# A MetaFormer block on one core: the attention's product with kv apart from wout, in column strips of PE, and all places of the convolution's work among the feed-forward chunks laid down anew

## The chip, the cores and the metric

One core of a Trainium2 chip. The metric is device microseconds of one execution: before, the median of three runs is 750.94 us (750.56 to 751.97). Everything is float32, or float32r where the kernel splits a number into a high and a low part.

## The reference, cut to what matters

x is 4 images of 96 channels and 56 x 56 pixels. A deformable attention with depthwise convolutions is added to x, then a mixture of experts over the pixels (all four experts are computed, the two best gates are kept).

```python
value = dwconv(xn, w_v, stride=1)
query = dwconv(xn, w_q, stride=1).reshape(B * 12, 32, 3136)
key   = dwconv(xn, w_k, stride=2).reshape(B * 12, 32, 784)
offset = gelu(layernorm(dwconv(xn, w_off1, stride=2))) @ w_off2
v_sampled = grid_sample(value, tanh(offset + ref)).reshape(B * 12, 32, 784)
attn = einsum('bcm,bcn->bmn', query, key) * SCALE      # no softmax
out  = einsum('bmn,bcn->bcm', attn, v_sampled)
x = x + einsum('bchw,oc->bohw', out, w_out)
t = tokens(x)
t = t + sum_e gate[e] * (gelu(layernorm(t) @ w1[e] + b1[e]) @ w2[e] + b2[e])
```

Without a softmax the attention of a head is query times the 32 x 32 matrix kv = key times v_sampled. The reshape puts 8 channels of four image quarters into the 32 "channels" of a head, so kv joins the four quarters, and is masked so that channels of different heads don't meet.

## The kernel before, in words

**Layout.** A picture's channels lie as 3 blocks of 32; a block's partitions are 4 quarters x 32 channels. `query[:, i, :]` is block i, 128 partitions by 784 pixels. There are 28 token tiles of 112 pixels, 7 groups of four of them (448 pixels) for the experts, 8 sample tiles of 98, and 8 strips of 392 pixels for the attention (two per quarter).

**Attention of batch b.** `sample` (DVE) weighs the gathered value rows into `vs`. `key_values` (PE) makes kv for each quarter q of the output, `mask_kv` (DVE) masks it, `mixes` (PE) multiplies it by wout: for each quarter three matrices `mix[:, q, i, :]` of 128 x 96, emptied by ACT. `attended` (PE) then makes each strip of y with three matmuls over the blocks, `add_y` (DVE) adds it to x, and `x1_to_tokens` (PE) turns it into tokens that ACT empties.

**Experts.** A chunk is 128 hidden units of one expert for 448 pixels: three float32r products into `ph` (L762 to L764), gelu on ACT (L1006), and the second product into `py` (L746). Three chunks make an output: DVE adds the bias and multiplies by the gate into one of four buffers `ye` (L1416), and POOL adds `ye` into x, the first 76 by an accumulating DMA (L1480). There are 84 chunks and 28 outputs per batch, 252 chunks in this form; the last 84 use split hidden values. The chunks of batch b-1 run while batch b is convolved.

**What sets the order.** Each engine has its own program, written out by hand: lists say how many chunks (`CHUNKS_AHEAD`, PE), gelus (`GELUS_AHEAD`, ACT), outputs (`OUTPUTS_AHEAD`, DVE) and sums (`SUMS_AHEAD`, POOL) stand ahead of each piece of the convolution's work. `chunks_to(plan.at("kv"))` issues chunks up to that number and then goes on. Each engine runs its program strictly in that order.

**Waits between them.** PE's second product of the first chunk of output n waits until output n-2 is made (two banks `py`):

```python
pe.wait_ge(ye_ready, FREE_OUTPUTS + n - 1)      # second(k), L745; k // 3 is n
```

DVE's output n waits until sum n-4 has landed (four buffers `ye`), and a sum waits for its output and for the sums before it:

```python
after_sums(dve, n + 1 - EXPERTS)                # outputs_to
pool.wait_ge(ye_ready, FREE_OUTPUTS + n + 1)    # add_outputs, L1476
after_sums(pool, n)
```

POOL also gathers the value rows for the samples, two indirect DMAs for each of 8 sample tiles (L1469), once the positions are known and the value table has been written to memory by DMA. The table is written after the last valT job; `values_to_tokens` makes valT with seven jobs on PE and ACT. POOL's loop over a batch, L1491 to L1495:

```python
for k in range(NS):
    add_outputs(added, SUMS_AHEAD[b][k])
    added = SUMS_AHEAD[b][k]
    gather(b, k)
```

SP loads the gates and stores the results (`load_gates`, `store_result`) behind the same semaphores. DVE's convolution taps (L1133) run over `xpad` in SBUF.

Of the kernel before, what the change touches and what calls it, by code (L numbers as in the profile page):

```python
# [35 lines left out]
SP = 98  # L36
# [31 lines left out]

def act_jobs():

    order = jobs(0, "xT", NG) + jobs(0, "pad", 2 * BLOCKS) + jobs(0, "offT", 2) + jobs(0, "valT", QT)[:VALUE_HALF] + jobs(0, "offc", 2) + jobs(0, "valT", QT)[VALUE_HALF:]
    order += jobs(1, "xT", NG)[:EARLY_SLOTS] + jobs(0, "keyT", 2) + jobs(1, "xT", NG)[EARLY_SLOTS:] + jobs(0, "mix", QUARTERS) + jobs(0, "x1T", NG) + jobs(1, "pad", 2 * BLOCKS)
    order += jobs(0, "gateT", 1) + jobs(1, "offT", 2) + jobs(1, "offc", 2)
    for b in range(1, BATCH):
        more = b + 1 < BATCH
        order += jobs(b, "valT", QT)
        if more:
            order += jobs(b + 1, "xT", NG)
        order += jobs(b, "keyT", 2)
        if more:  # L80
            order += jobs(b + 1, "pad", 2 * BLOCKS)
        order += jobs(b, "mix", QUARTERS) + jobs(b, "x1T", NG)
        if more:
            order += jobs(b + 1, "offT", 2)
        order += jobs(b, "gateT", 1)
        if more:
            order += jobs(b + 1, "offc", 2)
    return order


def dve_jobs():

    order = jobs(0, "offs", 1)
    for b in range(BATCH):
        order += jobs(b, "kv", QUARTERS) + jobs(b, "y", NY) + jobs(b, "x1c", NG)
        if b + 1 < BATCH:
            order += jobs(b + 1, "offs", 1)
# [17 lines left out]
SCALE_AFTER = 4  # L115
# [3 lines left out]
    dict(x1c=(0, 0, 0, 0, 3, 3, 4), gateT=(3,), offT=(10, 10), offc=(16, 16), offs=(18,)),  # L119
    dict(valT=(42, 42, 43, 43, 44, 44, 45), xT=(45, 46, 46, 47, 47, 48, 48), keyT=(49, 49),  # L120
         pad=(69, 69, 70, 71, 71, 72), kv=(72, 72, 73, 73), mix=(73, 73, 74, 74), y=(74, 74, 74, 74, 74, 74, 74, 74),
         x1T=(74, 74, 74, 74, 74, 74, 75), offT=(75, 76), x1c=(80, 80, 81, 82, 86, 86, 87), gateT=(86,), offc=(93, 93),
         offs=(95,)),
    dict(valT=(118, 118, 119, 119, 120, 120, 121), xT=(121, 122, 122, 123, 123, 124, 124), keyT=(125, 125),
         pad=(145, 145, 146, 147, 147, 148), kv=(148, 148, 151, 151), mix=(151, 151, 152, 152),
         y=(152, 152, 152, 152, 152, 152, 152, 152), x1T=(152, 152, 152, 152, 152, 152, 153), offT=(153, 154),
         x1c=(158, 158, 159, 160, 164, 164, 165), gateT=(164,), offc=(172, 172), offs=(174,)),
    dict(valT=(198, 198, 199, 199, 200, 200, 201), keyT=(204, 204), kv=(222, 226, 233, 233), mix=(233, 233, 234, 234),
         y=(234, 234, 234, 234, 234, 234, 234, 234), x1T=(234, 234, 234, 234, 234, 234, 235),
         x1c=(241, 241, 243, 243, 249, 249, 250), gateT=(249,)),  # L130
# [3 lines left out]
    dict(x1n=(0, 0, 0), x1c=(0, 0, 0, 0, 3, 3, 4), exp=(0,), gateT=(3,), offT=(10, 10), offc=(16, 17), tanh=(19,)),  # L134
    dict(valT=(42, 42, 43, 43, 44, 44, 45), xT=(45, 46, 46, 47, 47, 48, 48), keyT=(49, 49), xn=(67, 69, 69),
         pad=(69, 70, 70, 71, 71, 72), mix=(73, 73, 74, 74), x1T=(74, 74, 74, 74, 74, 74, 75), offT=(75, 76),
         x1n=(78, 80, 82), x1c=(80, 81, 83, 84, 86, 86, 87), exp=(81,), gateT=(86,), offc=(93, 94), tanh=(95,)),
    dict(valT=(118, 118, 119, 119, 120, 120, 121), xT=(121, 122, 122, 123, 123, 124, 124), keyT=(125, 125),
         xn=(143, 144, 145), pad=(145, 146, 146, 147, 147, 148), mix=(151, 151, 152, 152),
         x1T=(152, 152, 152, 152, 152, 152, 153), offT=(153, 154), x1n=(156, 158, 160),  # L140
         x1c=(158, 159, 161, 162, 164, 164, 165), exp=(159,), gateT=(164,), offc=(172, 173), tanh=(175,)),
    dict(valT=(198, 198, 199, 199, 200, 200, 201), keyT=(204, 204), mix=(233, 233, 234, 234),
         x1T=(234, 234, 234, 234, 234, 234, 235), x1n=(239, 241, 243), x1c=(241, 242, 245, 245, 249, 249, 250),
         exp=(243,), gateT=(249,)),
# [43 lines left out]
def build(nc, t, out):  # L188
# [4 lines left out]
    with ExitStack() as ctx:  # L193
# [11 lines left out]
        head_mask = sb("head_mask", [C, C])  # L205
# [290 lines left out]
        def _(pe):  # L496
# [127 lines left out]
            def key_values(b, quarters, before=lambda q: None):  # L624

                keyq = keyT[:, :, :].rearrange("p (q h) c -> p h q c", h=2)
# [8 lines left out]
            def mixes(b, before=lambda q: None):  # L635

                for q in range(QUARTERS):
                    before(q)
                    pe.wait_ge(dve_done, dved(b, "kv", q))
                    bank = act_bank(b, "mix", q)  # L640
                    for i in range(BLOCKS):
                        last = nc.tensor.matmul(bank[:, i * C:(i + 1) * C], kv[:, q, i, :, :].rearrange("d k c -> d (k c)"), wout[:, :], start=True, stop=True)
                    last.then_inc(act_full, 1)
# [51 lines left out]
            def first_rest(b, plan, chunks_to):  # L695
# [11 lines left out]
                key_values(b, range(QUARTERS))  # L707
                mixes(b)
# [8 lines left out]
            def rest(b, with_head, plan, chunks_to):  # L717
# [7 lines left out]
                key_values(b, range(QUARTERS), lambda q: chunks_to(plan.at("kv", q)))  # L725
                mixes(b, lambda q: chunks_to(plan.at("mix", q)))
# [811 lines left out]
```

## Time and profile before

| | |
|---|---|
| median of three runs | 750.94 us |
| profiled execution | a span of 749.4 us from the first to the last instruction; the page gives no other time of it |
| PE busy | 707.8 us (94%), mean granted clock 0.985 |
| DVE busy | 582.8 us (78%) |
| ACT busy | 384.5 us (51%) |
| POOL busy | 216.9 us (29%) |

Busy times of PE are modelled: shown matmuls overlap, and costs are better read from one start to the next. The stages are: batch 0 alone up to about 138 us, then three cycles of about 160 us (batches 1, 2 and 3 among the chunks of the batch before), and from about 637 us the last chunks alone.

### The profile page before, as it was taken

The numbers are of one execution on the slowest core, as the hardware profiler recorded it, in microseconds if no ns is written. First come the engines' busy times: TensorE is split into PE (matmuls) and PEld (weight loads), VectorE is DVE, ScalarE is ACT, GpSimd is POOL, SyncE is SP. The second block draws the span as 40 slices with busy tenths as digits, with TensorE's granted clock in tenths as the row PEclk, the third lists the DMA queues.
The fourth block names the chain that finished last, engine by engine and source line by source line (L and its number), as shares of the span: only waits on it lengthen the run. The fifth ranks groups of instructions, "written<-read, shape, count | busy, mean of one in ns | idle before, by whom it ended". The sixth has DMA issues, their size and how long they took to land.

```text
span 749.4 us, 9619 instructions
## 1 busy us (share of the span) xinstructions
PE 707.8 (94%) x3186; PEld 495.8 (66%) x3186; DVE 582.8 (78%) x1511; ACT 384.5 (51%) x722; POOL 216.9 (29%) x184
## 2 busy tenths in 40 slices
PE   5798999799999999999999999999998999999996
PEld 5556566566676666556767566666664665788884
DVE  4889648899999858699999477899975275677774
ACT  2314124744464614744556218545542256899995
POOL 4001700012128610111168201222285121344443
PEclk9998999799999999999999999999999999999999
DMA  8007200044464530345654422435645201121111
GB/s 195 9 0 198 53 9 1 7 98 86 89 185 115 98 56 10 68 103 119 155 129 83 86 48 46 82 80 101 190 102 109 35 20 49 47 69 51 66 47 37
DMA packets 29697, 58.66 MB, mean 78 GB/s; under 512 B 6224, under 2 KB 20176, under 8 KB 29360
## 3 DMA queue, kind: packets, MB, share of 16 engines
q0 software_dynamic: 11584, 17.90, 15.4%
q1 hardware_dynamic: 14336, 32.59, 14.7%
q10 hardware_dynamic: 3728, 7.55, 3.3%
q8 instruction: 26, 0.43, 0.2%
q14 instruction: 23, 0.19, 0.1%
HBM read 30.30 MB, written 14.65 MB: 60 GB/s over the span
## 4 chain that ended last, share of the span: by engine, by line
PE 56%; DVE 19%; DMA 7%; ACT 6%; POOL 5%; issue 5%; POOLq 0%; ACTq 0%
PE py L746 9%; PE pd L662 8%; PE ph L578 7%; DVE val L1133 6%; POOL big L1469 4%; DMA xbuf<-ye 4%; DVE query L1133 3%; PE pa L650 3%; PE pa L529 2%; PE ph L762 2%; PE ph L782 2%; PE ph L784 2%; PE ph L763 2%; PE ph L783 2%; PE ph L764 2%
## 5 line engine op out<-in xcount | busy, mean ns | idle before, releaser
L746 PE MATMUL py<-hid,w 128*96 128x448 f32 x504 | 234.4, 546 | 11.5 <-ACT hid L1006 8.7
L1006 ACT ACTIVATE hid<-ph,b 128x448 f32<-128x448 f32 x252 | 158.9, 632 | 148.1 <-PE ph L764 144.8
L762 PE MATMUL ph<-x_hi,w_hi 96*128 96x448 f32 x252 | 164.4, 653 | 0.0
L1480 POOL DMA_DIRECT2D xbuf<-ye x76 | 66.6, 877 | 327.2 <-DMA xbuf<-ye 163.2
L1469 POOL DMA_INDIRECT big<-value_table,rows x64 | 87.8, 1372 | 90.5 <-DVE rows L1193 56.5
L746 PEld LDWEIGHTS py<-hid,w 128*96 128x96 f32 x504 | 81.6, 165 | 31.2 <-ACT hid L1006 12.6
L763 PE MATMUL ph<-x_lo,w_hi 96*128 96x448 f32 x252 | 93.5, 371 | 0.0
L764 PE MATMUL ph<-x_hi,w_lo 96*128 96x448 f32 x252 | 92.8, 368 | 0.0
L1482 POOL TENSOR_TENSOR xbuf<-xbuf,ye 96x448 f32<-96x448 f32 x36 | 53.9, 1497 | 102.6 <-DVE ye L1416 99.9
L1416 DVE SCALAR_TENSOR_TENSOR ye<-py,b,gate_all 96x448 f32<-96x448 f32 x112 | 75.3, 674 | 9.3 <-PE py L746 7.3
L1443 DVE TENSOR_TENSOR hid_lo<-hid,hid_hi 128x448 fp32r<-128x448 f32 x84 | 59.7, 710 | 27.3 <-ACT hid L1015 27.1
L1133 DVE SCALAR_TENSOR_TENSOR query<-xpad,conv_w,query 128x784 f32<-128x784 f32 x80 | 78.3, 1027 | 0.5
L1133 DVE SCALAR_TENSOR_TENSOR val<-xpad,conv_w,val 128x784 f32<-128x784 f32 x80 | 78.3, 1026 | 0.4
L762 PEld LDWEIGHTS ph<-x_hi,w_hi 96*128 96x128 f32 x252 | 48.3, 192 | 41.1 <-issue 39.7
L763 PEld LDWEIGHTS ph<-x_lo,w_hi 96*128 96x128 f32 x252 | 48.8, 194 | 35.6 <-issue 35.0
L662 PE MATMUL pd<-query,mix_area 128*96 128x392 f32 x192 | 67.2, 493 | 0.0
L1015 ACT ACTIVATE hid_hi<-ph,b 128x448 fp32r<-128x448 f32 x84 | 53.3, 634 | 6.9 <-PE ph L784 1.7
L1015 ACT ACTIVATE hid<-ph,b 128x448 f32<-128x448 f32 x84 | 52.5, 625 | 0.0
L826 ACT ACTIVATE big<-pa 112x400 f32<-112x400 f32 x28 | 14.0, 502 | 70.6 <-PE pa L650 70.6
L764 PEld LDWEIGHTS ph<-x_hi,w_lo 96*128 96x128 f32 x252 | 47.9, 190 | 3.3
L662 PEld LDWEIGHTS pd<-query,mix_area 128*96 128x96 f32 x192 | 29.6, 164 | 23.9 <-issue 23.9
L1354 DVE TENSOR_TENSOR xbuf<-pd,xbuf 96x392 f32<-96x392 f32 x32 | 17.9, 560 | 32.8 <-PE pd L662 32.5
(165 smaller groups left out, 1081.2 us busy)
## 6 DMA issues: line engine op xcount, KB each, us to landing
gate_all<-gate_rows SPq DMA_DIRECT2D x56, 336.0 KB, 3.5
xbuf<-ye POOLq DMA_DIRECT2D x76, 168.0 KB, 3.4
value_table<-valT ACTq DMA_DIRECT2D x6, 1176.0 KB, 8.9
out<-xbuf SPq DMA_DIRECT2D x28, 168.0 KB, 2.0
xbuf<-in_x SPq DMA_DIRECT2D x3, 1176.0 KB, 10.1
value_table<-valT SPq DMA_DIRECT2D x2, 672.0 KB, 5.3
big<-value_table,rows POOLq DMA_INDIRECT x64, 2.8
value_table<-valT SPq DMA_DIRECT2D x2, 504.0 KB, 5.0
```

The source lines that it names most:

```text
L662: last = nc.tensor.matmul(bank[0:C, 0:YPIX], mix[:, q, i, :], query[:, i, h * YPIX:(h + 1) * YPIX], start=(i == 0), stop=(i == BLOCKS - 1))
L746: nc.tensor.matmul(py[e % 2][0:C, 0:GPIX], w2[:, c, :], hid[:, k % 3, :], start=(j == 0), stop=(j == CPE - 1)).then_inc(hid_used, 1)
L762: nc.tensor.matmul(bank, w1_hi[:, cols], xh(b, g), start=True, stop=False)
L763: nc.tensor.matmul(bank, w1_hi[:, cols], xl(b, g), start=False, stop=False)
L764: nc.tensor.matmul(bank, w1_lo[:, cols], xh(b, g), start=False, stop=True).then_inc(hid_full, 1)
L1006: nc.scalar.activation(hid[:, k % 3, :], ph[k % 2][:, 0:GPIX], ACT.Gelu, bias=b1[:, k % NCH:k % NCH + 1]).then_inc(hid_act, 1)
L1015: nc.scalar.activation(dst[:, k % 3, :], ph[k % 2][:, 0:GPIX], ACT.Gelu, bias=b1[:, k % NCH:k % NCH + 1]).then_inc(ready, 1)
L1133: ins = v.scalar_tensor_tensor(to, src, w, to, ALU.mult, ALU.add)
L1416: v.scalar_tensor_tensor(ye[0:C, e, :], py[e % 2][0:C, 0:GPIX], b2[:, e:e + 1], gate_all[0:C, e, :], ALU.add, ALU.mult).then_inc(ye_ready, 1)
L1443: v.tensor_tensor(hid_lo[:, m % 2, :], hid[:, k % 3, :], hid_hi[:, k % 3, :].bitcast(f32), ALU.subtract).then_inc(hid_lo_ready, 1)
L1469: p.indirect_dma_start(got[:, tile, r, :, :].rearrange("p a c -> p (a c)"), None, table, bass.IndirectOffsetOnAxis(ap=rows[:, r, tile:tile ...
L1480: pool.dma_start(to, ye[0:C, e, :], accum_op=ALU.add).then_inc(ye_summed, 16)
```

## The change

- `key_values` makes kv at once, with the key samples as the stationary side: 6 matmuls with 128 columns into one bank, of which the diagonal 32 x 32 squares of each block and quarter are wanted. `mask_kv` is one instruction. kv waits for all four quarters' samples. `keyT` is laid out by blocks.
- `mixes` goes, on PE and ACT. New is `attend`: for strip n three matmuls with 32 stationary columns, one per block, each into its own 32 partitions of one bank. ACT copies the 96 x 392 result into `att`, and one matmul with wout makes y. Attend n+1 is issued ahead of y n.
- DVE's waits for the mixes go, since kv has a buffer of its own.
- On ACT, batch 0 scales batch 1's tokens after all token copies and not among them.
- All numbers in the four lists are new. `SUMS_AHEAD` has one number for all eight tiles of a batch.

```diff
-                for q in quarters:
-                    before(q)
-                    pe.wait_ge(sampled, b * QUARTERS + q + 1)
-                    bank = dve_bank(b, "kv", q)
+                before(0)
+                pe.wait_ge(sampled, (b + 1) * QUARTERS)
+                bank = dve_bank(b, "kv")
+                for i in range(BLOCKS):
                     for h in range(2):
-                        last = nc.tensor.matmul(bank[0:C, 0:QUARTERS * C], vs[:, 2 * q + h, :], keyq[:, h], start=(h == 0), stop=(h == 1))
-                    last.then_inc(dve_full, 1)
...
+                        last = nc.tensor.matmul(bank[:, i * 128:(i + 1) * 128], keyT[:, h, i, :], vs[:, h:NS:2, i * CB:(i + 1) * CB], start=(h == 0), stop=(h == 1))
+                last.then_inc(dve_full, 1)
...
+            def attend(b, n):
+
+                q, h = n // 2, n % 2
+                if n == 0:
+                    pe.wait_ge(query_conv, b + 1)
+                    pe.wait_ge(dve_done, dved(b, "kv"))
+                bank = act_bank(b, "att", n)
+                for i in range(BLOCKS):
+                    last = nc.tensor.matmul(bank[i * CB:(i + 1) * CB, 0:YPIX], kv[:, i, q, :], query[:, i, h * YPIX:(h + 1) * YPIX], start=True, stop=True)
+                last.then_inc(act_full, 1)
...
+                before_att(0)
+                attend(b, 0)
                 for n in range(NY):
+                    if n + 1 < NY:
+                        before_att(n + 1)
+                        attend(b, n + 1)
                     before(n)
-                    pe.wait_ge(query_conv, b + 1)
-                    q, h = n // 2, n % 2
-                    pe.wait_ge(act_done, acted(b, "mix", q))
+                    pe.wait_ge(act_done, acted(b, "att", n))
                     bank = dve_bank(b, "y", n)
-                    for i in range(BLOCKS):
-                        last = nc.tensor.matmul(bank[0:C, 0:YPIX], mix[:, q, i, :], query[:, i, h * YPIX:(h + 1) * YPIX],
-                                                start=(i == 0), stop=(i == BLOCKS - 1))
-                    last.then_inc(dve_full, 1)
+                    nc.tensor.matmul(bank[0:C, 0:YPIX], wout[:, :], att[:, n % 2, :], start=True, stop=True).then_inc(dve_full, 1)
...
 SUMS_AHEAD = [(0, 0, 0, 0, 0, 0, 0, 0),
-              (15, 16, 17, 17, 18, 18, 19, 20),
-              (40, 41, 42, 42, 43, 43, 44, 44),
-              (67, 68, 69, 70, 70, 71, 71, 72)]
+              (15, 15, 15, 15, 15, 15, 15, 15),
+              (41, 41, 41, 41, 41, 41, 41, 41),
+              (68, 68, 68, 68, 68, 68, 68, 68)]
```

Chunks ahead on PE, before and after, for the places that the prediction uses:

| stage | place | before | after |
|---|---|---|---|
| batch 1 | valT, first to last | 42 to 45 | 44 to 47 |
| | tokens of batch 2 (xT) | 45 to 48 | 47 |
| | keyT | 49 | 47, 48 |
| | pads of batch 2 | 69 to 72 | 65 to 67 |
| | kv | 72, 72, 73, 73 | 69 |
| | last x1T | 75 | 72 |
| batch 2 | valT | 118 to 121 | 120 to 123 |
| | pads of batch 3 | 145 to 148 | 143 to 145 |
| | kv | 148, 148, 151, 151 | 147 |
| batch 3 | valT | 198 to 201 | 198 to 201 |
| | kv | 222, 226, 233, 233 | 224 |
| | last x1c | 250 | 242 |

## Rows read from the trace of the kernel before

**Rows 1.** Windows by batch: stretch, length, busy PE, PEld, DVE, ACT, POOL, clock, DMA
```profile
142.00:303.00 161.00, 159.93 (x729) 108.55 (x730) 141.17 (x376) 78.66 (x149) 45.66 (x42) 0.99 0.41 88
303.00:462.00 159.00, 154.56 (x710) 103.95 (x709) 134.52 (x361) 78.91 (x151) 45.37 (x42) 1.00 0.44 96
462.00:623.00 161.00, 154.53 (x649) 100.81 (x647) 120.27 (x295) 75.54 (x137) 51.41 (x44) 1.00 0.40 88
```

**Rows 2.** Timeline of PE, chunks in batch 2: start, length, instruction, tiles, shape, count
```profile
331.93 0.92 PE L746 MATMUL py<-hid,w 128*96 128x448 f32 x2
...
333.30 0.92 PE L746 MATMUL py<-hid,w 128*96 128x448 f32 x2
```

**Rows 3.** Timeline of PE, batch 0: tokens of batch 1, kv, mixes
```profile
94.52 4.15 PE L529 MATMUL pa<-ident_gate,xbuf 96*112 96x96 f32 x40
...
98.50 5.33 PE L632 MATMUL pd<-keyT,key_area 98*96 98x384 f32 x16
...
103.67 2.95 PE L642 MATMUL pa<-wout,kv_area 96*128 96x96 f32 x24
```

**Rows 4.** Timeline of PE, batch 3: one strip of y, then tokens
```profile
591.26 2.14 PE L662 MATMUL pd<-query,mix_area 128*96 128x392 f32 x6
593.24 0.94 PE L650 MATMUL pa<-ident_gate,xbuf 96*112 96x100 f32 x8
```

**Rows 5.** Timeline of DVE and ACT, batch 0: mask, first addition, token copy, last statistics
```profile
103.87 0.55 DVE L1348 TENSOR_TENSOR kv_area<-pd,head_mask 96x384 f32<-96x384 f32 x1 [0.74 <-PE pd L632]
...
108.63 0.56 DVE L1354 TENSOR_TENSOR xbuf<-pd,xbuf 96x392 f32<-96x392 f32 x1 [4.21 <-PE pd L662]
...
116.11 0.50 ACT L826 ACTIVATE big<-pa 112x400 f32<-112x400 f32 x1 [2.19 <-PE pa L650]
...
128.47 1.38 DVE L1082 BATCH_NORM_STATS2 st<-big 112x6 f32<-112x96 f32 x8 [0.66 <-ACT big L826]
```

**Rows 6.** Waits of PE, whole span: who waited for whom, us, times, longest
```profile
PE py L746 <- DVE ye L1416: 2.7, 3, 1.9
...
PE pd L632 <- DVE kv_area L1348: 1.1, 1, 1.1
```

**Rows 7.** Timeline around POOL's gathers: valT, first and last gathers, sums, taps, output
```profile
210.64 0.49 PE L621 MATMUL pa<-ident,val 128*112 128x128 f32 x3
...
223.27 1.38 POOL L1469 DMA_INDIRECT big<-value_table,rows  x1 [6.28 <-DMA value_table<-valT]
...
224.57 0.67 DVE L1416 SCALAR_TENSOR_TENSOR ye<-py,b,gate_all 96x448 f32<-96x448 f32 x1
224.95 4.01 POOL L1469 DMA_INDIRECT big<-value_table,rows  x1 [0.30 <-issue]
225.16 2.91 DVE L1133 SCALAR_TENSOR_TENSOR query<-xpad,conv_w,query 128x784 f32<-128x784 f32 x3
228.96 0.97 POOL L1480 DMA_DIRECT2D xbuf<-ye  x1
...
239.12 0.97 POOL L1469 DMA_INDIRECT big<-value_table,rows  x1 [0.30 <-issue]
...
255.89 0.96 POOL L1469 DMA_INDIRECT big<-value_table,rows  x1 [0.30 <-issue]
...
381.65 1.79 POOL L1469 DMA_INDIRECT big<-value_table,rows  x1 [0.30 <-issue]
...
412.88 0.97 POOL L1469 DMA_INDIRECT big<-value_table,rows  x1 [0.30 <-issue]
...
422.99 0.79 POOL L1480 DMA_DIRECT2D xbuf<-ye  x1 [3.10 <-DMA xbuf<-ye]
...
540.33 1.07 POOL L1469 DMA_INDIRECT big<-value_table,rows  x1 [9.22 <-DMA value_table<-valT]
...
572.01 0.97 POOL L1469 DMA_INDIRECT big<-value_table,rows  x1 [0.30 <-issue]
```

**Rows 8.** Windows: a stretch behind sparse work of PE, columns as in rows 1
```profile
138.00:142.00 4.00, 2.89 (x10) 2.10 (x8) 3.01 (x13) 3.96 (x10) 0.00 (x0) 0.50 0.00 0
```

More of the change, by code:

```diff
@@ L66, in jobs, with attended_jobs @@
     return [(b, name, g) for g in range(number)]
+def attended_jobs(b):
+    att, tokens = jobs(b, "att", NY), jobs(b, "x1T", NG)
+    order = att[:3]
+    for n in range(3, NY):
+        order += [att[n], tokens[n - 3]]
+    return order + tokens[NY - 3:]
 def act_jobs():
     order = jobs(0, "xT", NG) + jobs(0, "pad", 2 * BLOCKS) + jobs(0, "offT", 2) + jobs(0, "valT", QT)[:VALUE_HALF] + jobs(0, "offc", 2) + jobs(0, "valT", QT)[VALUE_HALF:]
-    order += jobs(1, "xT", NG)[:EARLY_SLOTS] + jobs(0, "keyT", 2) + jobs(1, "xT", NG)[EARLY_SLOTS:] + jobs(0, "mix", QUARTERS) + jobs(0, "x1T", NG) + jobs(1, "pad", 2 * BLOCKS)
+    order += jobs(1, "xT", NG)[:EARLY_SLOTS] + jobs(0, "keyT", 2) + jobs(1, "xT", NG)[EARLY_SLOTS:] + attended_jobs(0) + jobs(1, "pad", 2 * BLOCKS)
     order += jobs(0, "gateT", 1) + jobs(1, "offT", 2) + jobs(1, "offc", 2)
@@ L81, in act_jobs @@
             order += jobs(b + 1, "pad", 2 * BLOCKS)
-        order += jobs(b, "mix", QUARTERS) + jobs(b, "x1T", NG)
+        order += attended_jobs(b)
         if more:
@@ L94, in dve_jobs @@
     for b in range(BATCH):
-        order += jobs(b, "kv", QUARTERS) + jobs(b, "y", NY) + jobs(b, "x1c", NG)
+        order += jobs(b, "kv", 1) + jobs(b, "y", NY) + jobs(b, "x1c", NG)
         if b + 1 < BATCH:
@@ L114 @@
 KEYS_AHEAD = 9
-SCALE_AFTER = 4
 FIRST_SPLITS, GATES_AFTER = 2, 3
 CHUNKS_AHEAD = [
[L119 to L130, printed above, removed]
@@ L131 @@
+    dict(att=(225, 225, 226, 226, 226, 226, 226, 226), gateT=(240,), keyT=(205, 205), kv=(224,),
+         valT=(198, 198, 199, 199, 200, 200, 201), x1T=(226, 226, 226, 226, 226, 226, 227),
+         x1c=(232, 232, 234, 235, 240, 240, 242), y=(226, 226, 226, 226, 226, 226, 226, 226)),
 ]
 GELUS_AHEAD = [
[L134 to L144, printed above, removed]
+    dict(exp=(0,), gateT=(5,), offT=(11, 11), offc=(18, 18), tanh=(21,), x1c=(0, 0, 2, 3, 5, 6, 7), x1n=(0, 0, 2)),
@@ L145 @@
+    dict(att=(225, 225, 226, 226, 226, 226, 226, 226), exp=(234,), gateT=(240,), keyT=(205, 205),
+         valT=(198, 198, 199, 199, 200, 200, 201), x1T=(226, 226, 226, 226, 226, 226, 227),
+         x1c=(232, 233, 236, 237, 240, 240, 242), x1n=(231, 232, 236)),
 ]
 OUTPUTS_AHEAD = [
[12 rows of a table removed]
[12 rows of a table added]
 ]
 SUMS_AHEAD = [(0, 0, 0, 0, 0, 0, 0, 0),
[3 rows of a table removed]
[3 rows of a table added]
 Stats = namedtuple("Stats", "st sa sd sv si su mean rstd")
@@ L622, in values_to_tokens, with key_values @@
                     last.then_inc(act_full, 1)
-            def key_values(b, quarters, before=lambda q: None):
-                keyq = keyT[:, :, :].rearrange("p (q h) c -> p h q c", h=2)
-                for q in quarters:
-                    before(q)
-                    pe.wait_ge(sampled, b * QUARTERS + q + 1)
-                    bank = dve_bank(b, "kv", q)
-                    for h in range(2):
-                        last = nc.tensor.matmul(bank[0:C, 0:QUARTERS * C], vs[:, 2 * q + h, :], keyq[:, h], start=(h == 0), stop=(h == 1))
-                    last.then_inc(dve_full, 1)
[L635 to L640, printed above, removed]
-                    for i in range(BLOCKS):
-                        last = nc.tensor.matmul(bank[:, i * C:(i + 1) * C], kv[:, q, i, :, :].rearrange("d k c -> d (k c)"), wout[:, :], start=True, stop=True)
-                    last.then_inc(act_full, 1)
+            def key_values(b, before=lambda q: None):
+                before(0)
+                pe.wait_ge(sampled, (b + 1) * QUARTERS)
+                bank = dve_bank(b, "kv")
+                for i in range(BLOCKS):
+                    for h in range(2):
+                        last = nc.tensor.matmul(bank[:, i * 128:(i + 1) * 128], keyT[:, h, i, :], vs[:, h:NS:2, i * CB:(i + 1) * CB], start=(h == 0), stop=(h == 1))
+                last.then_inc(dve_full, 1)
             def x1_to_tokens(b, g):
@@ L706, in first_rest @@
                 x_to_tokens(b + 1, slots=range(EARLY_SLOTS, QT))
-                key_values(b, range(QUARTERS))
-                mixes(b)
+                key_values(b)
                 pe.wait_ge(conv_done, len(first_convs))
@@ L911, in values_to_tokens, with attend @@
                                          pa[bank][0:TP, 0:BLOCKS * 128].rearrange("p (i j c) -> p i j c", i=BLOCKS, c=CB), ACT.Copy).then_inc(act_done, 1)
-            def mixes(b, before=lambda q: None):
-                for q in range(QUARTERS):
-                    before(q)
-                    empty(b, "mix", q, mix[:, q, :, :], 128, BLOCKS * C)
+            def attend(b, n):
+                empty(b, "att", n, att[:, n % 2, :], C, YPIX)
             def x1_to_tokens(b, g):
@@ L963, in first_rest @@
                 x_to_tokens(b + 1, slots=range(EARLY_SLOTS, QT))
-                mixes(b)
-                act.wait_ge(dve_done, dved(b, "kv", QUARTERS - 1))
-                for g in range(NG):
+                for n in range(NY):
+                    attend(b, n)
+                    if n >= 3:
+                        x1_to_tokens(b, n - 3)
+                for g in range(NY - 3, NG):
                     x1_to_tokens(b, g)
-                    if g == SCALE_AFTER:
-                        scaled(b + 1)
+                scaled(b + 1)
                 padded(b + 1)
@@ L986, in rest @@
                     padded(b + 1, lambda g: gelus_to(plan.act_at("pad", g)))
-                mixes(b, lambda q: gelus_to(plan.act_at("mix", q)))
-                act.wait_ge(dve_done, dved(b, "kv", QUARTERS - 1))
-                for g in range(NG):
+                for n in range(NY):
+                    gelus_to(plan.act_at("att", n))
+                    attend(b, n)
+                    if n >= 3:
+                        gelus_to(plan.act_at("x1T", n - 3))
+                        x1_to_tokens(b, n - 3)
+                for g in range(NY - 3, NG):
                     gelus_to(plan.act_at("x1T", g))
@@ L1516 @@
         "ident": np.eye(128, dtype=f),
-        "head_mask": (ch[:, None] == ch[None, :]).astype(f),
+        "head_mask": np.tile((ch[:CB, None] == ch[None, :CB]).astype(f), (QUARTERS, 1)),
         "ref": ref.astype(f),
```

62 lines of the change are left out of this document (36 added, 26 removed), and 24 rows, old and new, of the table OUTPUTS_AHEAD.

## The prediction

> **What bounds the kernel now.** I read three views in this order. First the windows by batch: in each of the three cycles in which a batch's convolution and attention lie among the feed-forward chunks of the batch before, PE is busy 154.5 to 159.9 us of 159 to 161, DVE 120 to 141 and ACT under 79 [rows 1]. Then the timeline of PE: a chunk's second product starts 1.37 us after the one before it, with nothing between [rows 2]; the shown lengths overlap, so I take costs from start to start. Then the waits: only 3.8 us of PE's waits belong to the places that this change touches, 2.7 for the output buffer `ye` and 1.1 for the masked `kv` [rows 6]. So PE sets the end: a microsecond of PE work taken out comes off the span, and one in which PE waits goes on top. The sum below is made against the span of 749.4 us. The page gives no other time of that execution; the median of the runs is 750.94, so 1.5 us lie outside the span, and I add them at the end.
>
> **What the change takes out and adds on PE, per batch.** A float32 matmul is two passes in the trace.
> - `kv`: 16 passes of 384 columns take 5.17 us (from 98.50 to the first of the mixes at 103.67), 0.32 each [rows 3]. Now there are 12 passes of 128 columns, at the spacing of the mixes (24 in 2.95 less the 0.16 tail, 0.116 each) 1.4 us. Gain 3.8 us; between 3.4 and 4.2 for any row between.
> - The mixes go: 2.8 us [rows 3].
> - Per strip of 392 pixels, the three matmuls that gave y were 6 passes in 1.98 us (591.26 to 593.24), 0.33 each; the row shows 2.14, so a pass's tail is 0.16 [rows 4]. Now there are six passes with 32 stationary columns, into three disjoint column strips, and two passes with wout, 0.66. No matmul of before writes a part of the columns beside another, so the price of the six lies between 0.66 (the strips run beside each other and only the two passes of one strip follow each other) and 1.98 (all in a row). I take 0.66: nothing in the kernel makes one strip wait for another, and they write different partitions of one bank. Going over to strips and back, PE may have to empty: 0 to 0.16 each way, I take 0.16. That is 0.66 + 0.66 + 0.32 = 1.64 for 1.98, a gain of 0.34 a strip and 2.7 a batch.
>
> Sum 9.3 us for each of batches 1 to 3, 27.9 in all. The page "TensorE: Matmul & The Clock Gate" of the Trainium skill (Part 3) reports 2.38 times for three 32-column tiles, which would make the six passes 0.83. The same section says that matmuls start and end strictly in program order. No run here shows either. The second speaks against the change, since the two passes of one strip stand next to each other in the program; it is the second rival below.
>
> What lies beside it: ACT now empties eight tiles of 96x392 where it emptied four of 128x288; the nearest row is 0.50 us for 112x400 [rows 5], so 4 us for 1.6, under cover, as ACT is busy half of a cycle [rows 1]. Attend n+1 stands ahead of y n on PE, so ACT has 0.66 us for its 0.50 and the semaphores; in the first strip that misses by some 0.1, later strips have the token matmuls in between too. If that cover went, it would cost 8 x 0.2 a batch. DVE masks once instead of four times, each 0.55 [rows 5], and its off taps need not wait for the mixes: a gain for DVE, none on PE by itself.
>
> **Batch 0** has no chunks yet, so its chain counts and not PE's sum. kv starts where it did (98.5). Then 1.4, the mask 0.6, two attends and ACT's copy 1.3, y 0.8, semaphores 0.4: the first addition at about 103.1 instead of 108.63 [rows 5]. From there DVE is nearly full to the last statistics at 129.85 in before; it stays so. ACT now scales batch 1 after all token copies (3.3 us later in its queue than where `SCALE_AFTER` had it), which delays its part of the normalising, but fewer x1c come ahead of chunk 0. I take the whole 5.5 us, bounds 2 and 8.
>
> **The sums behind the gathers: the large term.** `SUMS_AHEAD` is now the same number for all eight tiles (15, 41, 68). POOL's order then is: sums up to there, sixteen gathers without a sum between, and only then the next sum. The outputs behind it: DVE's output n waits for sum n-4 (four `ye` buffers), and PE's second product of the first chunk of output n waits for output n-2. Counted from 0, 15 sums let DVE go to output 18 and stop PE at output 21, that is chunk 63; 41 stop it at chunk 141, 68 at chunk 222. The new places show the same: pads and scaling of batch 2 stand at 65, those of batch 3 at 143, kv of batch 3 at 224, just behind. So PE has a fixed stock of work from the last valT to the stop, and waits for what is left of POOL's round.
> - The round: the first gather stands 12.3 us after the last valT transposes (210.97 to 223.27, the table's DMA). Then the sixteen gathers. Then a sum: 0.97 to issue, 3.1 to land, and 0.67 for the output [rows 7]. Together 17.0 + G.
> - G, the sixteen gathers alone: in before they took 33.6, 32.2 and 32.65 us in batches 1 to 3 from the first start to the last end, with five, four and five sums between, each 0.97 and 0.31 to the next: without them 27.2, 27.1 and 26.2 [rows 7]. The lower bound is 16 x 1.27 = 20.3, the spacing at 239.12. I take the three measured ones, because the slow gathers are those beside DVE's query taps (4.01 us beside a run of three taps [rows 7]) and these taps remain.
> - PE's stock: batch 1, valT ends at 47, so 17 chunks of 1.37, a first product 0.6, the tokens of batch 2 (56 passes; 40 took 4.0 [rows 3]) 5.6, keyT about 1: 30.5. Batch 2, from 123: 19 chunks, 33.2. Batch 3, from 201, no tokens: 22 chunks, 31.7.
> - The wait: 44.2 - 30.5 = 13.7, 44.1 - 33.2 = 10.9, 43.2 - 31.7 = 11.5; sum 36.1. With G at 20.3 it is 16.5; with three more gathers a batch caught by the taps (3 x 1.3) 48. Queued behind the waiting product is all of PE's program: pads, kv, attention; behind the waiting output on DVE stands the sampling, and SP's stores and gate loads wait for the same sums and outputs. In before POOL put a sum after nearly every tile, and this wait was 2.7 us.
> - After such an idle stretch the clock falls: at 138 to 142, behind sparse work, the granted clock was 0.50, the 1.2 GHz level [rows 8]; those 4 us lost 2. Three times 1.7, 5 us; 0 to 12.
>
> The page "SBUF — State Buffer" of the Trainium skill (the part on engine ports) says that DVE and GpSimd share a port pair as an exclusive lock, and that a GpSimd operation which reads SBUF is shut out by a DVE operation with two SBUF inputs. The trace agrees as far as it goes: 4.01 us beside taps, 0.96 beside statistics. By that rule alone G would not shrink with the sums gone.
>
> **The sum.** 749.4 - 27.9 (batches 1 to 3) - 5.5 (batch 0) - 3.8 (old waits at these places, replaced) + 36.1 + 5 = 753.3 of span, 755 us with the 1.5 around it.
>
> **Rivals.**
> 1. The gathers run free once nothing stands between them: G = 20.3. For it: 0.96 to 1.05 us each wherever DVE does not run taps. Against it: half the time of the first gathers lies beside taps in all three batches. Waits 16.5, span 734, time 735, faster than before. It decides where G is under about 25.5 on average: each microsecond of G counts three times, and four have to go.
> 2. The passes of a strip follow each other in program order and hold up the next strip: strip 0 first, strip 0 second beside strip 1 first, and so on, four slots of 0.33 instead of two. 0.66 x 24 = 15.8 more: 771. For it: PE's passes start in program order in every row of before. Against: strips are separate parts of the array.
> 3. The strips don't run beside each other at all, so that the change doesn't do what it says: 1.32 x 24 = 31.7 more and some 4 in batch 0: 790. For it: nothing in before overlaps by more than the 0.16 tail.
> 4. PE never reaches the stop, because the convolution's chain is later than its new places and PE waits or works elsewhere: 36.1 and 5 fall away, 714. Against: the stock is fixed by PE's own order, and the table's DMA by PE's valT.
>
> **How the numbers follow.** Forecast 0.45, with its own range of 745 to 764 (clock 0 to 12, drains 0 to 0.16, batch 0); rival 1 0.17; rival 2 0.15; rival 3 0.13; rival 4 0.06; the rest, 0.04, other new waits, slower. Faster or slower by 0.2% is about what a measurement of this kernel can tell from none: under 749.4 or over 752.4. Faster: rivals 1 and 4 and some 0.07 of the forecast's, 0.30. Same: 0.06, all of it from the forecast. Slower: 0.64. The range from 731 to 777 takes in rivals 1 and 2 and leaves out 3 and 4, 0.2.
>
> **What would show it.** Right: PE's second product waits three times for `ye`, 11 to 14 us each, at chunks 63, 141 and 222; POOL shows sixteen gathers in a row, 26 us or more; the granted clock is half just after. Strips right: six passes of attend within 0.7 to 0.9 us from the first start to the wout product; 1.3 means rival 2, 2.0 rival 3. kv's passes at 0.11 and no line of the mixes. Wrong: PE's waits for `ye` are below 20 us in all, or PE's waits moved to the convolution's chain (kv, x1c), which would mean that DVE and not the sums sets the pace.

## The result, and the profile after

The changed kernel takes 764.88 us (median of 4 runs, 763.66 to 766.52) against 750.75 us of the kernel before on the same chip: 1.8% slower, ratio 1.0181 with a 95% interval of 1.0136 to 1.0226. The profiled execution has a span of 762.2 us and a mean granted clock of 0.943; the kernel before had 749.4 us and 0.985.

The first view is the windows by batch, the same stretches as the second and third of [rows 1]: PE's busy time fell by 11 us in each, and the clock fell too.

```profile
303.00:462.00 159.00, 143.72 (x689) 96.86 (x688) 130.84 (x355) 79.88 (x150) 44.23 (x41) 0.96 0.43 93
462.00:623.00 161.00, 143.32 (x632) 93.35 (x631) 120.27 (x297) 77.07 (x142) 47.61 (x44) 0.94 0.41 90
```

Next PE's waits (us in total, times, longest). What was 2.7 us [rows 6] is now 48.7; the wait for the gelu's `hid` shrank by 6.0 us (the first fence is before, the second after).

```profile
PE py L746 <- ACT hid L1006: 8.7, 7, 1.8
```

```profile
PE py L751 <- DVE ye L1421: 48.7, 4, 16.7
...
PE py L751 <- ACT hid L1014: 2.7, 5, 0.7
```

PE's timeline gives the three large ones, 46.4 us together, at the first chunk of outputs 21, 47 and 74: chunks 63, 141 and 222.

```profile
259.17 1.78 PE L751 MATMUL py<-hid,w 128*96 128x448 f32 x2 [15.55 <-DVE ye L1421]
...
421.74 1.78 PE L751 MATMUL py<-hid,w 128*96 128x448 f32 x2 [14.11 <-DVE ye L1421]
...
584.13 1.78 PE L751 MATMUL py<-hid,w 128*96 128x448 f32 x2 [16.72 <-DVE ye L1421]
```

POOL's timeline of batch 1 shows what stands behind the first of them: sixteen gathers in a row from 224.44 to 254.70 (30.3 us; 28.8 in batches 2 and 3), the first five of them 1.7 to 4.0 us long, then the sum, whose landing lets DVE make output 19 at 258.34 (line not shown), the one that PE's second product of output 21 waits for.

```profile
224.44 3.00 POOL L1474 DMA_INDIRECT big<-value_table,rows  x1 [11.54 <-DMA value_table<-valT]
227.74 1.66 POOL L1474 DMA_INDIRECT big<-value_table,rows  x1 [0.30 <-issue]
229.71 4.03 POOL L1474 DMA_INDIRECT big<-value_table,rows  x1 [0.30 <-issue]
234.04 3.11 POOL L1474 DMA_INDIRECT big<-value_table,rows  x1 [0.31 <-issue]
237.46 3.12 POOL L1474 DMA_INDIRECT big<-value_table,rows  x1 [0.30 <-issue]
240.89 0.97 POOL L1474 DMA_INDIRECT big<-value_table,rows  x1 [0.30 <-issue]
...
253.73 0.97 POOL L1474 DMA_INDIRECT big<-value_table,rows  x1 [0.30 <-issue]
254.71 0.98 POOL L1485 DMA_DIRECT2D xbuf<-ye  x1
```

Behind the wait the clock is at half (the third figure from the right; columns as in [rows 1]), and PE works through some 6.3 us of it before it is back: the windows around the first wait.

```profile
246.00:249.00 3.00, 0.00 (x0) 0.00 (x0) 2.73 (x11) 1.27 (x5) 2.39 (x3) 0.91 0.20 58
...
258.00:261.00 3.00, 1.83 (x4) 0.99 (x5) 2.66 (x11) 0.00 (x0) 0.83 (x1) 0.50 0.59 146
261.00:264.00 3.00, 3.00 (x14) 2.77 (x14) 1.48 (x7) 1.09 (x3) 0.00 (x0) 0.50 0.78 194
264.00:267.00 3.00, 3.00 (x16) 2.13 (x15) 1.97 (x8) 1.50 (x3) 0.78 (x1) 0.75 0.11 16
```

Last, PE's timeline of a strip, before and then after, and of kv after. From start to start a strip's six attend passes take 0.79 us, the two with wout 0.73 and the twelve of kv 1.25; a strip with its tokens takes 2.39 where it took 2.76.

```profile
274.91 2.14 PE L662 MATMUL pd<-query,mix_area 128*96 128x392 f32 x6
276.89 0.94 PE L650 MATMUL pa<-ident_gate,xbuf 96*112 96x100 f32 x8
277.67 2.14 PE L662 MATMUL pd<-query,mix_area 128*96 128x392 f32 x6
```

```profile
286.11 0.94 PE L646 MATMUL pa<-ident_gate,xbuf 96*112 96x100 f32 x8
286.98 0.86 PE L657 MATMUL pa<-query,kv 128*32 128x392 f32 x6
287.77 0.90 PE L671 MATMUL pd<-att_area,wout 96*96 96x392 f32 x2
288.50 0.94 PE L646 MATMUL pa<-ident_gate,xbuf 96*112 96x100 f32 x8
...
433.25 1.50 PE L638 MATMUL pd<-key_area,keyT 98*128 98x128 f32 x12
434.50 0.45 PE L767 MATMUL ph<-x_hi,w_hi 96*128 96x448 f32 x1
```

### The profile page after: what moved, and what is told of

Read it like the earlier page. It is cut to its first block, busy times and chain, and to the rows that moved or that the text cites. A ratio compares the mean times of both kernels' runs of the same rounds, so it can differ in the third digit from the quotient of the medians.

```text
span 762.2 us, 9497 instructions
## 1 busy us (share of the span) xinstructions
PE 680.4 (89%) x3138; PEld 474.6 (62%) x3138; DVE 576.2 (76%) x1499; ACT 394.4 (52%) x738; POOL 215.2 (28%) x184
## 4 chain that ended last, share of the span: by engine, by line
PE 60%; DMA 12%; POOL 10%; DVE 7%; ACT 6%; issue 4%; POOLq 0%; ACTq 0%; DVEq 0%
PE py L751 14%; POOL big L1474 10%; DMA xbuf<-ye 10%; PE ph L585 7%; PE ph L767 3%; PE ph L768 3%; PE ph L769 3%; PE pa L657 3%; PE pd L671 3%; DVE val L1141 3%; PE pa L646 2%; PE pa L536 2%; PE ph L787 2%; PE ph L788 2%; PE ph L789 2%
## 5 line engine op out<-in xcount | busy, mean ns | idle before, releaser
L751 PE MATMUL py<-hid,w 128*96 128x448 f32 x504 | 237.6, 553 | 51.4 <-DVE ye L1421 48.7
L1485 POOL DMA_DIRECT2D xbuf<-ye x76 | 61.7, 812 | 361.3 <-DMA xbuf<-ye 198.7
L1474 POOL DMA_INDIRECT big<-value_table,rows x64 | 92.3, 1442 | 87.4 <-DVE rows L1201 57.0
L767 PEld LDWEIGHTS ph<-x_hi,w_hi 96*128 96x128 f32 x252 | 48.7, 193 | 43.6 <-issue 43.1
L536 PE MATMUL pa<-ident_gate,xbuf 96*112 96x96 f32 x224 | 30.2, 307 | 6.3 <-DMA xbuf<-in_x 5.4
L1141 DVE SCALAR_TENSOR_TENSOR key_area<-xpad,conv_w,key_area 128x196 f32<-128x196 f32 x96 | 34.8, 418 | 1.0
L1141 DVE SCALAR_TENSOR_TENSOR kv_area<-xpad,conv_w,kv_area 128x196 f32<-128x196 f32 x96 | 34.5, 413 | 0.4
L536 PEld LDWEIGHTS pa<-ident_gate,xbuf 96*112 96x112 f32 x224 | 29.4, 219 | 6.9 <-issue 5.5
```

Of the source, the lines that this page charges most:

```text
L536: last = nc.tensor.matmul(bank[0:TP, j * C:(j + 1) * C], x_of(b)[:, t0:t0 + TP], ident_gate[:, 0:C], start=True, stop=True)
L751: nc.tensor.matmul(py[e % 2][0:C, 0:GPIX], w2[:, c, :], hid[:, k % 3, :], start=(j == 0), stop=(j == CPE - 1)).then_inc(hid_used, 1)
L767: nc.tensor.matmul(bank, w1_hi[:, cols], xh(b, g), start=True, stop=False)
L1141: ins = v.scalar_tensor_tensor(to, src, w, to, ALU.mult, ALU.add)
L1474: p.indirect_dma_start(got[:, tile, r, :, :].rearrange("p a c -> p (a c)"), None, table, bass.IndirectOffsetOnAxis(ap=rows[:, r, tile:tile ...
L1485: pool.dma_start(to, ye[0:C, e, :], accum_op=ALU.add).then_inc(ye_summed, 16)
```

## The experiments

The theory: sixteen gathers with no sum between them hold the outputs, and PE waits for them; the attention itself is faster. Its rivals: the strips are no faster; or another gate (the convolution's chain, DVE's order) would hold PE at the same places without the block.

**1. The block alone, in the kernel before** (e2).

```diff
-              (15, 16, 17, 17, 18, 18, 19, 20),
-              (40, 41, 42, 42, 43, 43, 44, 44),
-              (67, 68, 69, 70, 70, 71, 71, 72)]
+              (15, 15, 15, 15, 15, 15, 15, 15),
+              (41, 41, 41, 41, 41, 41, 41, 41),
+              (68, 68, 68, 68, 68, 68, 68, 68)]
```

> The kernel before with only its sums taken out from between the gathers (15, 41, 68 for all eight tiles), attention as it was. Theory A, the sums alone make PE stop at chunks 63, 141 and 222: the round is 17.0 us and about 29.5 of gathers, PE's work up to the stop about 32, 34.5 and 32 us, so waits of 14, 12 and 14 us and 2 us of clock behind each, 790 us. Rival, the gathers run at 1.27 us each when nothing stands between them: three waits of 3 to 5 us, 763 us. Rival, another wait of the same place is only taken over: 751 us.

798.63 us, ratio 1.0624 (1.0575 to 1.0674): theory A, 9 us above its 790, and 48 us from three lines of a list. PE's three waits are there, 33.8 us in sum; the other 14 us weren't divided, but PE also works at half clock behind the waits there (0.50 from 250 to 260 us):

```profile
256.83 1.78 PE L746 MATMUL py<-hid,w 128*96 128x448 f32 x2 [12.42 <-DVE ye L1416]
...
433.92 1.78 PE L746 MATMUL py<-hid,w 128*96 128x448 f32 x2 [10.01 <-DVE ye L1416]
...
609.54 1.78 PE L746 MATMUL py<-hid,w 128*96 128x448 f32 x2 [11.32 <-DVE ye L1416]
```

The sixteen gathers took 28.8, 27.6 and 28.7 us here. So a sum between them cost about 1 us in the kernel before (33.6, 32.2, 32.65 with five, four and five; 0.8 to 1.15 each), not the 1.28 that the prediction subtracted.

**2. One strip instead of three, in the changed kernel** (e4).

```diff
-    last = nc.tensor.matmul(bank[i * CB:(i + 1) * CB, 0:YPIX], kv[:, i, q, :], ...
+    last = nc.tensor.matmul(bank[0:CB, 0:YPIX], kv[:, i, q, :], ...
```

> The changed kernel with the three attend products of a strip all put into the first 32 partitions (so the attended values of the other two blocks are left out), the same passes and columns. If the strips run beside each other, a strip's six passes now follow each other at 0.33 us: 2.0 us for the 0.80 of the changed kernel, 1.2 more in 24 strips and up to 9 in batch 0, 790 to 803 us. If the passes are short for another reason (32 stationary columns), 765 us.

801.15 us, 36 us more than the changed kernel and within the 790 to 803 expected of strips that run beside each other. The same six passes now take 2.09 us from start to start, 0.35 each, where they took 0.79:

```profile
300.50 2.16 PE L657 MATMUL pa<-query,kv 128*32 128x392 f32 x6
302.59 0.90 PE L671 MATMUL pd<-att_area,wout 96*96 96x392 f32 x2
```

The strips do run beside each other; being narrow saves nothing. (All six passes now also write the same part of the bank, and the run doesn't tell a shared strip from a shared target.) The ratio of the two, 2.65, is somewhat above the 2.38 that the Trainium skill reports in "TensorE: Matmul & The Clock Gate" (Part 3).

**3. The sums between the gathers again, in the changed kernel** (e1, and e7 again).

```diff
-              (15, 15, 15, 15, 15, 15, 15, 15),
-              (41, 41, 41, 41, 41, 41, 41, 41),
-              (68, 68, 68, 68, 68, 68, 68, 68)]
+              (15, 16, 17, 17, 18, 18, 19, 19),
+              (41, 41, 42, 42, 43, 43, 44, 44),
+              (67, 68, 69, 70, 70, 71, 71, 72)]
```

> The changed kernel with sums put between the gathers again (15 to 19, 41 to 44, 67 to 72 over the eight tiles). Theory A, the sixteen gathers without a sum are the whole loss: PE's three waits for ye (46.4 us) and some 3 us of clock go, 716 us. Theory B, the loss moves on: the gathers still end where they did (DVE's taps hold the first six), the last sample is ready at about 260, 416 and 576 us, and PE now comes to kv earlier than that by some 6, 4 and 15 us and waits there, 742 us. Theory C, DVE's pace and not the sums holds PE: 760 us or more.

747.82 us, ratio 0.9947 (0.9921 to 0.9973), nearest to the 742 of theory B. The rows are those of e7, the same kernel once more. PE still waits for `ye`:

```profile
252.92 1.78 PE L751 MATMUL py<-hid,w 128*96 128x448 f32 x2 [6.41 <-DVE ye L1421]
...
404.62 1.78 PE L751 MATMUL py<-hid,w 128*96 128x448 f32 x2 [4.38 <-DVE ye L1421]
...
570.09 1.78 PE L751 MATMUL py<-hid,w 128*96 128x448 f32 x2 [18.89 <-DVE ye L1421]
```

29.7 us are left of 46.4 (theory B had some 25), now behind DVE's own list: `OUTPUTS_AHEAD` puts outputs 19, 45 and 72 behind the norm of the next batch and the sampling. So theory B's size is about right and its place is wrong: it had the wait at kv. The next run (e5) moved those outputs ahead, here told in words for batch 1; the two other batches are changed alike:

```diff
-  OUTPUTS_AHEAD, batch 1, from the last query tap: 19 (x10), 20 (x4), 21, 21, 22, 22, ...
+  19 (x3), 20 (x5), 21, 21, 22 (x8), ...
```

> The kernel with the sums between the gathers (its three waits for ye, 6.4, 4.3 and 19.2 us, now stand behind outputs 19, 45 and 72, which VectorE's list puts behind the norm or the sampling), with those outputs moved ahead among the samples, as in the kernel before; all other places as changed. Theory A, VectorE's list was the last gate: the waits for ye fall under 8 us in all and 722 to 728 us come out. Theory B, the samples are no sooner, and kv at chunks 69, 147 and 224 stands too early for them: PE waits the same 25 to 30 us, at kv instead of ye, 745 to 750 us.

760.14 us: no gain at all. The waits are where theory B put them, 25.4 us at kv and 8.9 at the pads, but the time is 10 us above its 745 to 750. To set the two side by side they ran once more on one chip:

> The changed kernel with sums between the gathers once more, beside the three others of this series on one chip: its median was 748 us while its profiled execution took 760, and the same kernel with outputs moved ahead among the samples 760. Theory A, outputs ahead among the samples change nothing by themselves (waits at ye become waits at pads and kv): both come out equal within 4 us. Theory B, outputs held behind the norm and the sampling are the better order, since VectorE reaches the normalising, which the pads wait for, some 6 us sooner: 748 us here, with pads that don't wait, and 757 to 760 us for the other.

> The kernel with sums between the gathers and outputs ahead among the samples once more, on the same chip. Theory A: equal to the one with outputs held back within 4 us. Theory B: 9 to 12 us longer than it, with waits of PE for the normalised tokens (6 and 3 us before the pads of batches 2 and 3) and for the samples (4, 4 and 17 us before kv).

748.70 us (ratio to before 0.9968, 0.9933 to 1.0004) with the outputs held back and 756.89 us (1.0052, 1.0011 to 1.0093) with them ahead, theory B of this pair, though the 8.2 us between them are a little under its 9 to 12 and the two intervals only just part. In e8 PE waits 34.6 us, at the pads for the normalised tokens and at kv for the samples:

```profile
249.14 0.68 PE L539 MATMUL pa<-ident,xT 112*128 112x56 f32 x2 [5.93 <-DVE xT L1104]
264.10 2.93 PE L636 MATMUL pd<-key_area,keyT 98*128 98x128 f32 x12 [3.78 <-DVE key_area L1342]
...
407.00 0.43 PE L539 MATMUL pa<-ident,xT 112*128 112x56 f32 x2 [2.98 <-DVE xT L1104]
422.44 2.93 PE L636 MATMUL pd<-key_area,keyT 98*128 98x128 f32 x12 [4.86 <-DVE key_area L1342]
...
577.31 2.93 PE L636 MATMUL pd<-key_area,keyT 98*128 98x128 f32 x12 [17.02 <-DVE key_area L1342]
```

So the new places of pads and kv come before their inputs are ready by 30 to 35 us in all, whichever instruction PE happens to wait at. In the changed kernel the block of gathers hides this: PE is held earlier, for longer.

**4. The new attention with the old lists** (e3, and e11 again): places, outputs and sums of the kernel before, kv where its last quarter stood, att where y stands.

```diff
-         kv=(72, 72, 73, 73), mix=(73, 73, 74, 74), y=(74, ...
+         kv=(73,), att=(74, 74, 74, 74, 74, 74, 74, 74), y=(74, ...
```

> The new attention (masked kv in strips, wout apart) with the places, outputs and sums of the kernel before; kv where its last quarter was. Theory A, the PE work taken out comes off the span: 9.3 to 10.5 us a batch and 1 to 5 us in batch 0, 716 to 722 us. Theory B, PE comes earlier to waits that were covered (ye behind the gathers, kv behind the samples), which give back some 5 us a batch: 733 to 738 us. Rival, the new attention costs more somewhere off PE (ACT's eight copies, mask in one piece): 745 us or more.

> The new attention at the old places once more, as the neighbour of the next kernel: 724 to 730 us, waits for ye of about 6 us, all in batch 3 at 544 to 564 us.

726.85 us, ratio 0.9647 (0.9590 to 0.9704), and 728.25 us, 0.9685 (0.9642 to 0.9727): faster than both kernels, between A and B. The span of e11's profile, 722.3 us, is 27.1 under that of the kernel before. Of the 9.7 us of PE's work taken out per batch (next part), 8.1, 9.5 and 7.5 us came off between the starts of the same chunks (42, 120, 198 and 251); what comes ahead of chunk 42 gave 2.7. In batch 3, which gave back 2.2, PE comes sooner to the outputs behind the gathers (the lines below); what took 1.6 us in batch 1 wasn't separated:

```profile
544.02 0.96 PE L795 MATMUL py<-hid,w 128*96 128x448 f32 x2 [1.75 <-DVE ye L1465]
550.15 0.96 PE L795 MATMUL py<-hid,w 128*96 128x448 f32 x2 [1.82 <-DVE ye L1465]
556.43 0.96 PE L795 MATMUL py<-hid,w 128*96 128x448 f32 x2 [1.97 <-DVE ye L1465]
```

**5. What makes the gathers slow** (e6): three query taps left out.

```diff
-                    query_tap(b, k)
+                    if k not in (5, 6, 7):
+                        query_tap(b, k)
```

> The changed kernel with query taps 5, 6 and 7 left out in batches 1 to 3 (9 of VectorE's 0.97 us instructions a batch, those beside the first gathers; the query is then not the whole convolution). Theory A, a gather takes over 2 us only beside VectorE's taps: the taps end some 8.7 us earlier, two or three slow gathers are left instead of six, and the sixteen take 23 to 25 us instead of 28.9 to 30.3; each wait for ye is 5 to 6 us shorter, 748 us. Rival, the first gathers are slow by themselves: sixteen in 29 to 30 us and 765 us.

747.87 us, ratio 0.9940 (0.9913 to 0.9967). The gathers took 25.2, 23.6 and 23.2 us for 30.3, 28.8 and 28.8, and PE's three waits 10.3, 8.8 and 10.9 for 15.6, 14.1 and 16.7. In batches 2 and 3 the first gathers now lie beside the gap in the taps and follow each other at 1.3 us:

```profile
539.07 1.07 POOL L1475 DMA_INDIRECT big<-value_table,rows  x1 [0.30 <-issue]
540.44 1.02 POOL L1475 DMA_INDIRECT big<-value_table,rows  x1 [0.30 <-issue]
541.76 0.96 POOL L1475 DMA_INDIRECT big<-value_table,rows  x1 [0.30 <-issue]
```

That is theory A. The gathers fell by 15.9 us, the waits by 16.4 and the time by 17.0: as the kernel stands a microsecond of the gathers counts on the end, and the taps set their length. The run also takes 8.7 us of DVE's work out of each batch, so 17.0 is not the price of the gathers alone. The Trainium skill says in "SBUF — State Buffer" (the part on engine ports) that a DVE instruction with two SBUF inputs and a GpSimd operation that reads SBUF shut each other out. The gathers, 3 to 4 us beside taps and 1 us in the gap, agree with it, taking the issue of a gather, which has its row numbers in SBUF, as such an operation; no run here shows the lock itself.

**6. Batch 0's clock** (e9): idle products in the new attention with the old lists, at four places behind the strips of batch 0; one of the four is shown.

```diff
+            def idle_products(n):
+                for k in range(n):
+                    nc.tensor.matmul(ph[k % 2][:, 0:128], ident[:, :], ident[:, :], start=True, stop=True)
...
+                quarters_back(b + 1, lambda g: idle_products(2))
```

> The new attention at the old places, with 36 more products of the identity into an unused bank on PE in the idle stretches of batch 0 between the last strips and chunk 0 (0.23 us each), nothing else. Theory A, in batch 0 it is PE's half clock from about 123 to 143 us that gives the time saved back: the clock stays at full, chunk 12 comes 2 to 4 us earlier, 723 to 725 us. Rival, the statistics and splits on VectorE and ScalarE set the pace there: chunk 12 where it was, 727 us, or 1 to 2 us more for the products.

727.62 us, ratio 0.9710 (0.9653 to 0.9768): the rival. From 120 to 136 us the clock was full with the products and 0.58 without (the first fence is e9, the second e11), yet chunk 12 came at 158.66 us with them and at 158.44 without. The executions didn't reach batch 0's kv at the same time (97.88 and 99.01 us); counted from there chunk 0 came after 37.0 us with the products and 36.7 without, and chunk 12 after 60.8 and 59.4. PE's clock was not what batch 0 waited for.

```profile
120.00:136.00 16.00, 14.73 (x132) 14.28 (x132) 9.37 (x41) 12.36 (x35) 0.00 (x0) 1.00 0.01 2
```

```profile
120.00:136.00 16.00, 11.95 (x66) 10.60 (x67) 10.09 (x45) 11.93 (x33) 0.00 (x0) 0.58 0.00 1
```

**7. Two tries at batch 3's waits**, both on the new attention with the old lists: sums and outputs one place sooner (e10), and one more sum with everything from kv on three chunks later (e12).

```diff
-              (67, 68, 69, 70, 70, 71, 71, 72)]
+              (67, 69, 70, 70, 71, 71, 72, 73)]      (e10; outputs 73, 74, 75, 76 among the samples)
+              (67, 68, 69, 70, 71, 71, 72, 73)]      (e12; kv=(236,))
```

> The new attention at the old places, with batch 3's sums and outputs each one place sooner among gathers and samples (67, 69, 70, 70, 71, 71, 72, 73). Theory A, PE's 6.1 us of waits for ye at 544 to 564 us stand behind outputs that are only queued behind samples: most of them and of the half clock behind them go, 721 to 723 us. Rival, one more sum among the gathers makes kv and the rest 1.3 us later: 727 to 728 us.

> The new attention at the old places, with one more sum among batch 3's gathers and everything of batch 3 from kv on three chunks later (kv at 236). Theory A, a sum costs POOL about 1 us and lets PE do three chunks, 4.1 us: PE's waits of 6 us before kv shrink to 2 or 3, 3 to 5 us less than its neighbour, 720 to 724 us. Rival, the three chunks are missing behind kv, where the last x1c have nothing to be hidden behind any more: equal to its neighbour or up to 4 us longer.

732.67 us (0.9772, 0.9721 to 0.9824), longer than either case allowed, and 730.33 us (0.9710, 0.9653 to 0.9767), the rival: no gain from either. In e10 the waits for `ye` are nearly gone (1.7 us in all), and 7.4 us stand at kv instead; the last sample is no sooner (560.9 us there, 554.2 in e11 and 561.7 in e3):

```profile
562.38 2.93 PE L682 MATMUL pd<-key_area,keyT 98*128 98x128 f32 x12 [7.40 <-DVE key_area L1388]
```

In e12 the waits for `ye` stay (5.4 us for 6.4), and PE's waits for the split x1 rise from 2.0 to 3.6 us. No version tried beats e3 by more than the runs of one kernel differ.

## Why the prediction was right

The likeliest case came true: the time lies 10 us above its 755, and 1 us above its own range of 745 to 764.

- **PE's work, batches 1 to 3.** Forecast 9.3 us a batch. kv takes 1.25 (forecast 1.4), the mixes' 2.8 are gone. (Per head, query has 784 positions, and key and v_sampled 196 each, which are the two tiles of 98 in kv's rows; the lengths in the reference as printed above are four times these.) A strip with its tokens went from 2.76 to 2.39, a gain of 0.37 for 0.34: attend 0.79 with its mode change, wout 0.73, and 0.09 more for the token matmuls behind it. 3.9 + 2.8 + 2.95 = 9.7 a batch, 29 us for 27.9. Rivals 2 and 3, 1.3 and 2.0 us of attend, fell at 0.79; e4, with 2.09, shows what rival 3 would have looked like.
- **Batch 0.** The first addition came at 103.11 us, forecast 103.1, and chunk 0 at 133.49 for 138.30: 4.8. By chunk 12 only 1.2 of it was left (160.03 for 161.21), at chunk 42 it was 2.0. The step that failed is "From there DVE is nearly full ...; it stays so. I take the whole 5.5": what follows the first addition (gates, splits, normalising) doesn't start earlier by as much. e9 rules out the clock of PE's idle stretch. Counted from the start of batch 0's kv, the first addition is 5.4 us sooner than before, with old lists and new. Chunk 12 comes at 62.7 us in the kernel before, at 59.4 with the new attention and the old lists (e11), and at 61.7 in the changed kernel: 2.1 us are lost with either lists, by which of these steps wasn't separated, and 2.3 more by the new lists. The rows show where the 2.3 went: the new lists issue the last three pieces of x1 at chunks 5 to 7, where it was 3 and 4; DVE splits them before it makes the first two outputs, at 151.03 us. So PE waits 2.34 us for `ye` (0.50 in the kernel before, 0.49 in e11), and the clock, 1.00 there in the kernel before and in e11, falls behind it.

```profile
151.85 0.96 PE L751 MATMUL py<-hid,w 128*96 128x448 f32 x2 [2.34 <-DVE ye L1421]
```

```profile
152.00:156.00 4.00, 4.00 (x10) 2.49 (x10) 3.89 (x12) 0.64 (x1) 0.94 (x1) 0.61 0.58 132
```

- **PE's stock.** 31.3, 34.0 and 32.3 us from the start of the last valT transposes to the stop; forecast, from their end 0.3 us later, 30.5, 33.2, 31.7.
- **The round** is the term that was mis-sized: 44.2, 44.1, 43.2 forecast, 46.9, 48.1 and 49.0 measured (counted like the stock, so 0.3 more than by the forecast's start), and 46.4 us of waits for 36.1. Two parts. G was 30.3, 28.8, 28.8 for 27.2, 27.1, 26.2, which is 7.4 us: 4.6 because a sum between gathers costs 1 us and not 1.28 (e2: 28.8, 27.6, 28.7), perhaps since part of it falls into time in which the gather would have stood beside a tap anyway; 2.8 came with the places of the changed kernel. The other part is the lead from the last valT to the first gather. Counted as in the forecast it was 11.8, 14.6 and 15.4, where I used batch 1's 12.3 for all. There POOL was still at the last sum ahead of the block (below). The kernel before had 14.9 and 14.3 in batches 2 and 3 already (from 366.72 and 526.03 to the first gathers of [rows 7]), so this could have been read ahead of the change.
- **The clock behind the waits.** PE worked 6.3, 4.3 and 5.2 us at half, 7.9 lost; forecast 5, range to 12.
- **A wait not in the sum:** PE's waits for `hid` fell from 8.7 to 2.7 us, with the new places of the chunks: it is 8.0 with the new attention at the old places (e11). The forecast owes part of its nearness to this: the waits were 10.3 us longer than in its sum, and these 6.0, of which it knew nothing, went the other way. That is luck.

With the measured sizes: 749.4 - 29.0 - 2.0 - 3.8 - 6.0 + 46.4 + 7.9 = 762.9; the span is 762.2. Some 1.7 us of the old waits lie before chunk 42 and so count twice, so the sum is good to 2 or 3 us and not to 0.7.

- **Rival 1** (gathers at 20.3) is out, e6 shows why: it would need the taps gone. **Rival 4** (PE never reaches the stop) is out in this kernel, but half of it was nearer than 0.06 said: without the block PE does run into waits at the convolution's chain, 30 to 35 us of them (e7, e8), so they would not have fallen away as its 714 has it.

What the forecast didn't see: that 46.4 us of waits aren't 46 us of the block's price. From 750.7 (to 752.9 on the chips of these runs), the strips give 24 (e3); the new places and outputs take back 21 to 33 (e1, e7, e8 and e5); the block takes another 16 on top of e7. In the kernel before, whose places fit its chain, the same three lines cost 48.

## What to carry to other kernels

A wait of the bounding engine has a second gate behind it: take the first away and look where the engine stops next before its length is called a gain. Where a bounding engine's stalls sit in front of one late input (here the last sample), moving work within that queue changed the name of the wait and gained nothing (e10; in e8 it cost 8 us); what is left is to make the input sooner, which no run here did without leaving work out. Three more chunks put in front of it gained nothing either (e12). When a block is cleared of small insertions, don't subtract their own length from its duration: measure the block without them. In e2 leaving out a sum saved 1 us where its length and gap are 1.28.

## What was not expected of the hardware

Not only gathers seem to stand behind DVE's taps: a sum's DMA on POOL may too. In the changed kernel, output 67 was done at 543.7 us and the sum before it had been issued 10 us ahead of the next, but sum 67 came only at 549.73, 0.2 us behind the end of a run of six taps. The first fence is DVE, the second POOL.

```profile
543.04 0.68 DVE L1421 SCALAR_TENSOR_TENSOR ye<-py,b,gate_all 96x448 f32<-96x448 f32 x1
543.63 5.88 DVE L1141 SCALAR_TENSOR_TENSOR query<-xpad,conv_w,query 128x784 f32<-128x784 f32 x6
```

```profile
549.73 0.79 POOL L1485 DMA_DIRECT2D xbuf<-ye  x1 [9.36 <-DMA xbuf<-ye]
550.83 3.05 POOL L1474 DMA_INDIRECT big<-value_table,rows  x1 [0.30 <-issue]
```

The wait is read from these rows alone; no run moved the taps away from that sum. As its end the profile names the landing of the sum before, issued at 539.57, so it may be that landing which came late and not the issue. And three strips of 32 columns do six passes in the time of 2.3 (0.79 against 0.35 each), though the two passes of a strip stand next to each other in the program: the order of starts that rival 2 feared didn't hold the strips up.
